# DLRM tower: first MLP layer spread over two steps, scale and offset at the turned copy, dense part of two blocks computed ahead

## The chip, the cores and the metric

The kernel runs on one core of a Trainium2 chip. Time is device time of one execution in microseconds (us), smaller is better. The core has TensorE (PE, with its weight loads as PEld), VectorE (DVE), ScalarE (ACT), GpSimd (POOL) and SyncE (SP), which only issues transfers here. Each engine works through its own instructions in the order in which they are written and waits on semaphores.

## The reference

A recommendation model on 512 samples, all in fp32. Cut to what matters (`ln` is layer norm over the last axis):

```
e = 26 table lookups per sample                              # [512, 26, 64]
x = ln(dense @ Wd.T) * gd + bd                               # [512, 128]
y = ln(e @ Ws.T) * gs + bs ; y = ln(y mixed by Wsi) * gsi + bsi   # 32 features of 128
T = [x, y]            ; Z = T @ T.T  (33 x 33 per sample), lower triangle
z = ln(Z_flat @ Wl.T) * gl + bl, the first 384 of 512 columns kept
h = relu([z, dense] @ W_top1 + b_top1)                       # 384 + 256 -> 512
h = relu(h @ W_top2 + b_top2)                                # 512 -> 256
out = h @ W_top3                                             # 256 -> 1
```

gl, bl and the biases are drawn, not ones and zeros.

## The kernel before

The 512 samples are 4 blocks of 128 (numbered k = 0 to 3, LAST = 3), and a block is 4 units of 16 pairs of samples, so there are 16 units, n = 0 to 15. GpSimd gathers the table rows of all units by 104 indirect transfers, six for a unit, eight for units 0, 4, 8 and 12. It waits for nothing but the indices.

All other engines run a software pipeline of steps n = 0 to 16, written out by hand. In step n TensorE does `transposes(n)` (L318) and `gram(n)` (L325), which give the row variances of unit n, `mix(n-1)` (L341) and `embed(n-1)` (L351) of the unit before, and `interact(n-2)` (L364, 32 small matmuls a unit). VectorE answers with L755 to L761 and L766 to L770 (`srow`, which `mix` waits for) and with L779 to L794 for the normalised T. ScalarE copies and squares between them; `interactions` (L595, L597) copies Z to `zs`. Z leaves through DRAM (L275 to L277) and comes back transposed (L241 to L250) before the block's `upper` layer, six matmuls of 512 columns called j = 0 to 5 (L381 to L386), can run. In fp32 every matmul is issued as two passes, which the profile counts one by one.

After `upper(k)`: `upper_norm` and `upper_scaled` (L614 to L622, the reciprocal L799 on VectorE) give `un`; `turn` (L392) transposes it on TensorE; `upper_turned` (L628) copies it as `znT`; `hidden1_dense` (L408, 8 matmuls) and `hidden1` (L422, in the last block L416, 12 matmuls) add up the first MLP layer in PSUM; `relu1` (L636), `hidden2` (L434), `relu2` (L642), `answer` (L444) follow. The scale gl is multiplied into W_top1 beforehand (`w1g`, L836), and the offset bl goes into the bias (`b1p`, L480 and L841), in step 6.

Where these stand is given by lags: `block_at(n, lag)` is block k when n = 4 k + lag, for blocks 0 and 1 alone. Their `upper` is in steps 4 k + 7 and 8, turn and first layer in 4 k + 9 (step 13 for block 1), second layer in 4 k + 10, answer in 4 k + 11. Blocks 2 and 3 are written out. `upper(2)` is cut over steps 15 and 16; what follows `interact(15)` is the tail:

```python
hidden1_dense(LAST - 1)
turn(LAST - 1)
hidden1_dense(LAST)
hidden1(LAST - 1)
upper(LAST, range(0, NL + 1))
hidden2(LAST - 1)
turn(LAST)
answer(LAST - 1)
hidden1(LAST)
```

`upper(3)` in it needs the last units' Z back from DRAM.

Of the kernel before, what the change touches and what calls it, by code (L numbers as in the profile page):

```python
# [11 lines left out]
P = 128  # L12
# [46 lines left out]
def build(nc, tables, index, consts, small, ws_t, gs_row, wsi_rows, dense_t, wd_t, wl, wlx, w1, w2, out):  # L59
# [3 lines left out]
    with ExitStack() as ctx:  # L63
# [55 lines left out]
        w1g = sb("w1g", [P, USED // P, H1])  # L119
        b1p = sb("b1p", [P, H1 // P])  # L120
# [75 lines left out]
        w1_ready, b1_done, b1_ready = map(sem, ["w1_ready", "b1_done", "b1_ready"])  # L196
# [111 lines left out]
        def _(pe):  # L308
# [59 lines left out]
            def upper(k, part):  # L368

                if part[0] == 0:  # L370
                    if k and k != LAST:
                        pe.wait_ge(h2_sb, H2 // P * k)
                    pe.wait_ge(zr_sb[k % 2], 16 * READS * (k // 2 + 1))
                    pe.wait_ge(xrow_sb, k + 1)
                    if k == 0:
                        pe.wait_ge(b1_ready, 1)
# [17 lines left out]

            def hidden1_dense(k):

                if k < LAST - 1:
                    pe.wait_ge(zT_sb, k + 1)
                else:
                    pe.wait_ge(t1_sb, 2 * NU)  # L400
                if k == LAST:
                    pe.wait_ge(zs_sb, NU)
                    pe.wait_ge(u_sb, LAST)
                if k == 0:
                    pe.wait_ge(w1_ready, 1)
                for c in range(USED // P, NK):
                    for m in range(H1 // P):
                        mm(hidden_part(k, m), w1_sb[:, c, P * m:P * (m + 1)], dense_sb[:, c - USED // P, P * k:P * (k + 1)],  # L408
                           start=c == USED // P and (m == 0 or k == LAST), stop=False, skip_group_check=True)

            def hidden1(k):
                pe.wait_ge(zT_sb, k + 1)
                if k == LAST:
                    for m in range(H1 // P):
                        for c in range(USED // P):
                            got = mm(hidden_part(k, m), w1g[:, c, P * m:P * (m + 1)], znT[:, c, :],  # L416
                                     start=False, stop=c == USED // P - 1, skip_group_check=True)
                        got.then_inc(h1_done, 1)
                else:
                    for c in range(USED // P):  # L420
                        for m in range(H1 // P):
                            got = mm(hidden_part(k, m), w1g[:, c, P * m:P * (m + 1)], znT[:, c, :],  # L422
                                     start=False, stop=c == USED // P - 1, skip_group_check=True)
                            if c == USED // P - 1:
                                got.then_inc(h1_done, 1)
# [48 lines left out]
            def hidden_bias():  # L474

                pe.wait_ge(ld_w1, 16 * NK)
                pe.wait_ge(w9_ready, 1)
                for m in range(H1 // P):
                    for c in range(USED // P):
                        got = mm(pU[:, m:m + 1], w1_sb[:, c, P * m:P * (m + 1)], col["bl"][:, c:c + 1],  # L480
                                 start=c == 0, stop=c == USED // P - 1)
                got.then_inc(b1_done, 1)

# [16 lines left out]
            for n in range(NU + 1):  # L500
# [16 lines left out]
                if (k := block_at(n, MLP)) is not None:  # L517
                    turn(k)
# [10 lines left out]
                if n == 6:  # L529
                    hidden_bias()  # L530
# [18 lines left out]
            upper(LAST, range(0, NL + 1))  # L549
            hidden2(LAST - 1)  # L550
# [7 lines left out]
        def _(act):  # L558
# [65 lines left out]
            def upper_turned(k):  # L624
# [3 lines left out]
                a.copy(znT[:], turn_bank(k)[:, 0:USED].rearrange("p (c n) -> p c n", n=P)).then_inc(zT_sb, 1)  # L628

            def relu1(k):  # L630
                if k == 0:
                    act.wait_ge(b1_ready, 1)
                for m in range(H1 // P):
                    if m == 0 or k == LAST:
                        act.wait_ge(h1_done, H1 // P * k + (m + 1 if k == LAST else H1 // P))
                    a.activation(h1[:, m, :], hidden_part(k, m), ACT.Relu, bias=b1p[:, m:m + 1]).then_inc(h1_sb, 1)  # L636
# [40 lines left out]
            for n in range(NU + 1):  # L677
# [12 lines left out]
                if (k := block_at(n, TOP)) is not None:  # L690
                    relu1(k)
# [6 lines left out]
                if n < NU:  # L698
                    row_deviation(n)
                if n == 0:  # L700
# [5 lines left out]
                if (k := block_at(n, MLP)) is not None:  # L706
                    upper_turned(k)
# [3 lines left out]
                if n >= 2:  # L711
                    interactions(n - 2)
                if (k := block_at(n, U0 - 1)) is not None:
# [17 lines left out]
            relu1(LAST - 1)  # L731
            upper_norm(LAST)
            upper_scaled(LAST)
            relu2(LAST - 1)
            upper_turned(LAST)
# [6 lines left out]
        def _(dve):  # L742
# [90 lines left out]
            def hidden_weights():  # L833
                dve.wait_ge(ld_w1, 16 * ((USED + DENSE) // P))
                for c in range(USED // P):
                    got = v.tensor_scalar(w1g[:, c, :], w1_sb[:, c, :], col["gl"][:, c:c + 1], None, ALU.mult)  # L836
                got.then_inc(w1_ready, 1)

            def hidden_bias():
                dve.wait_ge(b1_done, 1)  # L840
                v.tensor_tensor(b1p[:], pU[:, 0:H1 // P], col["b1"], ALU.add).then_inc(b1_ready, 1)  # L841
# [48 lines left out]
            for n in range(NU + 1):  # L890
                if n < NU:
                    row_variance(n)
                if (k := block_at(n, MLP)) is not None:
# [13 lines left out]
                if n == 6:  # L907
                    hidden_weights()
                    hidden_bias()
            upper_inverse(LAST - 1)  # L910
            upper_inverse(LAST)

# [66 lines left out]
```

## Time and profile before

| what | value |
|---|---|
| median of 3 runs | 182.81 us (182.76 to 183.86) |
| the profiled execution's own time | 184.26 us |
| its span | 182.5 us |
| mean granted TensorE clock | 0.972 |
| busy: PE / DVE / ACT / POOL | 146.5 / 117.0 / 86.0 / 106.0 us |
| last gather issued (L302) | ends 140.5 us from the start |

The span is what the trace covers, the profiled execution's own time lies 1.76 us above it, and the median of the runs without a profile is 1.45 us below that own time. Positions such as "at 166.29" are us from the start of the span. A timeline row gives start, duration, engine, line, operation, output and inputs, how many were merged in the row, and in brackets how long the engine had been idle before it and what ended that. A row of the page's groups gives line, engine, operation and count, then busy us and mean ns of one, then the idle time in front of them and what ended it.

### The profile page before, as it was taken

Reading aid. Unit: us, or ns where it says so; the run is one execution under the profiler, and the core shown is the slowest. Engines: PE = TensorE matmul, PEld = TensorE weight load, DVE = VectorE, ACT = ScalarE, POOL = GpSimd, SP = SyncE. Lnnn points to the kernel's source line nnn. Section 1 sums busy time; section 2 is a strip of 40 time slices with the busy share of each in tenths; the row PEclk is TensorE's granted clock in tenths of the full one; section 3 lists DMA queues with packets and bytes.
Section 4 is the critical chain, followed back from the end, with each engine's and each line's share of the span. In section 5 each row is a group of like instructions: output and inputs, shape, how many; then the busy total and the mean of one; then the engine's idle time right before and its main releaser. Section 6 shows DMA issues by size and latency. Waiting matters only on the chain.

```text
span 182.5 us, 4658 instructions
## 1 busy us (share of the span) xinstructions
PE 146.5 (80%) x1865; PEld 103.4 (57%) x1865; DVE 117.0 (64%) x279; ACT 86.0 (47%) x229; POOL 106.0 (58%) x108
## 2 busy tenths in 40 slices
PE   0475585648496989896996999699799999799995
PEld 0364263334162657764555977465497955497674
DVE  3798508797629899994869279939772996700000
ACT  3001333575425675773466176527634863712262
POOL 2778777787777777777777777777776000000000
PEclk9999969999969999799999999999999999999999
DMA  5613241325166653312136322212543103322000
GB/s 146 202 25 81 84 135 31 83 29 197 24 194 157 100 67 50 54 32 53 34 68 72 71 30 59 56 29 57 75 71 47 36 0 62 44 46 28 0 4 0
DMA packets 38520, 12.01 MB, mean 66 GB/s; under 512 B 34113, under 2 KB 35265, under 8 KB 38498
## 3 DMA queue, kind: packets, MB, share of 16 engines
q1 hardware_dynamic: 33586, 8.24, 20.6%
q0 software_dynamic: 3328, 3.41, 10.4%
q8 instruction: 15, 0.25, 0.5%
q10 hardware_dynamic: 1584, 0.05, 0.5%
q14 instruction: 7, 0.06, 0.1%
HBM read 9.46 MB, written 2.23 MB: 64 GB/s over the span
## 4 chain that ended last, share of the span: by engine, by line
POOL 51%; PE 20%; issue 16%; DMA 5%; DVE 3%; ACT 3%; SPq 1%; ACTq 0%; DVEq 0%
POOL rows L302 51%; PE pV L341 3%; PE pA L381 2%; PE pT L351 2%; PE pU L381 2%; DMA zr<-zscr 2%; DMA rows<-in_tables,idx 2%; PE pA L325 1%; PE pU L422 1%; PE pZ L364 1%; PE pU L408 1%; DMA idx_in<-in_index 1%; PE pU L434 1%; DMA zscr<-zs 1%; DVE T L794 1%
## 5 line engine op out<-in xcount | busy, mean ns | idle before, releaser
L302 POOL DMA_INDIRECT rows<-in_tables,idx x104 | 105.8, 1017 | 34.3 <-issue 31.4
L755 DVE TENSOR_TENSOR prod<-pA,rows 128x384 f32<-128x384 f32 (+1 forms) x16 | 9.4, 590 | 32.1 <-PE pA L325 32.1
L318 PE MATMUL pA<-const,rows 128*128 128x128 f32 x52 | 9.2, 294 | 18.3 <-DMA rows<-in_tables,idx 18.3
L794 DVE TENSOR_TENSOR T<-t,trs 128x512 f32<-128x512 f32 x32 | 22.2, 695 | 1.1
L583 ACT ACTIVATE t<-t 128x512 f32<-128x512 f32 x32 | 19.5, 629 | 6.2 <-DVE t L779 5.8
L341 PE MATMUL pV<-wexp,srow 128*64 128x192 f32 (+4 forms) x256 | 21.9, 317 | 0.0
L779 DVE TENSOR_TENSOR t<-pT,bias 128x512 f32<-128x512 f32 x32 | 20.5, 683 | 1.5 <-PE pT L351 1.4
L325 PE MATMUL pA<-gbd,rowsT 128*128 128x128 f32 x104 | 18.6, 326 | 3.5 <-ACT rowsT L566 3.4
L318 PEld LDWEIGHTS pA<-const,rows 128*128 128x128 f32 x52 | 5.9, 147 | 26.1 <-issue 23.2
L785 DVE TENSOR_REDUCE tss<-t 128x16 f32<-128x512 f32 x32 | 20.4, 677 | 0.1
L341 PEld LDWEIGHTS pV<-wexp,srow 128*64 128x64 f32 x256 | 16.5, 146 | 4.9 <-issue 3.3
L351 PE MATMUL pT<-vsb,wscg 64*128 64x512 f32 x64 | 19.0, 673 | 0.0
L325 PEld LDWEIGHTS pA<-gbd,rowsT 128*128 128x128 f32 x104 | 15.2, 222 | 6.6 <-ACT rowsT L566 4.3
L364 PEld LDWEIGHTS pZ<-T 128*32 128x32 f32 x1024 | 11.6, 109 | 11.5 <-issue 9.2
L566 ACT COPY rowsT<-pA 128x384 f32<-128x384 f32 (+1 forms) x16 | 7.9, 495 | 18.9 <-PE pA L318 18.9
L364 PE MATMUL pZ<-T 128*32 128x34 f32 x1024 | 13.7, 199 | 1.0 <-DVE T L794 1.0
L572 ACT ACTIVATE esd<-evar,eps 128x6 f32<-128x6 f32 (+1 forms) x16 | 4.8, 299 | 19.0 <-DVE evar L761 18.9
L588 ACT ACTIVATE tsd<-tss,eps 128x16 f32<-128x16 f32 x32 | 9.9, 308 | 6.9 <-DVE tss L785 6.6
L381 PE MATMUL pU<-wg,zr 128*128 128x512 f32 x24 | 13.0, 657 | 0.0
L578 ACT COPY vsb<-pV 128x512 f32<-128x512 f32 x16 | 9.4, 586 | 7.5 <-PE pV L341 7.1
L799 DVE RECIPROCAL urs<-usd 128x1 f32<-128x1 f32 x4 | 0.6, 160 | 14.4 <-ACT usd L616 14.3
L770 DVE TENSOR_TENSOR srow<-rows,ers 128x384 f32<-128x384 f32 (+1 forms) x16 | 9.5, 592 | 0.6
(153 smaller groups left out, 204.9 us busy)
## 6 DMA issues: line engine op xcount, KB each, us to landing
zscr<-zs SPq DMA_DIRECT2D x16, 128.0 KB
rows<-in_tables,idx POOLq DMA_INDIRECT x104, 2.6
wl_sb<-in_wl SPq DMA_DIRECT2D x5, 256.0 KB, 2.8
w_sb<-in_w SPq DMA_DIRECT2D x5, 256.0 KB, 3.4
dense_sb<-in_dense_t SPq DMA_DIRECT2D x1, 512.0 KB, 4.5
w_sb<-in_w SPq DMA_DIRECT2D x1, 512.0 KB
zr<-zscr SPq DMA_DIRECT2D x3, 96.0 KB
const<-in_consts SPq DMA_DIRECT2D x1, 263.0 KB, 2.9
```

The costliest lines, as they stand in the source:

```text
L302: pool.indirect_dma_start(out=rows[:, j, h * D:(h + 1) * D], out_offset=None, in_=tables, in_offset=bass.IndirectOffsetOnAxis(ap=idx[:, 2 ...
L318: got = nc.tensor.transpose(pA[n % 2][:, P * j:P * (j + 1)], rows[:, first + j, :], ident)
L325: got = mm(pA[n % 2][:, P * j:P * (j + 1)], rowsT[:, n % 2, j, :], gbd[:], start=True, stop=True)
L341: got = mm(pV[(n - m + u) % 2][D * h:D * (h + 1), PJ * (a - US * u):PJ * (z + 1 - US * u)], srow[:, n % 2, i, D * h:D * (h + 1)], wexp[:, ...
L351: mm(pT[h][:], wscg[D * h:D * (h + 1), :], vsb[D * h:D * (h + 1), n % 2, :], start=True, stop=True).then_inc(y_done, 1)
L364: got = mm(pZ[PJ * s:PJ * (s + 1), NCOL * g:NCOL * (g + 1)], t[:, h, i, 0:PJ], t[:, h, i, :], start=True, stop=True)
L381: mm(upper_bank(k)[:], zr[:, k % 2].rearrange("p a (g j) -> p (a g) j", j=4)[:, :, j], wg[:, j, :], start=j == 0, stop=False)
L583: a.activation(t2[:, h], t1[:, n % 2, h], ACT.Square).then_inc(t_sq, 1)
L588: a.activation(tsd[:, h], tss[:, h], ACT.Sqrt, bias=eps[:], scale=1.0 / PJ).then_inc(t_std, 1)
L779: v.tensor_tensor(t1[:, n % 2, h], pT[h][:].rearrange("p (a b) -> p a b", b=PJ), bias[:].unsqueeze(1).to_broadcast([P, US, PJ]), ALU.add). ...
L785: v.tensor_reduce(out=tss[:, h], in_=t2[:, h], op=ALU.add, axis=AX.X).then_inc(t_var, 1)
L794: v.tensor_tensor(tile_T(n)[:, h, :, 0:PJ], t1[:, n % 2, h], trs[:, h].unsqueeze(2).to_broadcast([P, US, PJ]), ALU.mult).then_inc(t_sb, 1)
```

## The change

1. **First layer, blocks 0 and 1.** `hidden1(k)` is cut: of the three 128-row chunks c of znT the first stays in step 4 k + 9 behind the dense part, the other two (8 matmuls) move to step 4 k + 10, between `gram` and `embed`. `turn(k)` goes behind `interact`. On ScalarE `upper_turned` goes behind `interactions`, and `relu1` behind `row_deviation`.
2. **Scale and offset.** `w1g` and `b1p` go, with the 12 small matmuls and the 4 VectorE instructions that made them. The copy to znT becomes three ScalarE activations of 128x128 with scale gl and offset bl (blocks 0 to 2), or three VectorE tensor_scalar (`last_turned`, block 3).
3. **Dense part of blocks 2 and 3.** It is computed in step 6 (`dense_ahead(0)` ahead of `embed(5)`, `dense_ahead(1)` behind `interact(4)`, 8 matmuls each) and stored in `hd`. VectorE adds it in four instructions a block (`hidden_sum`, to `hs`) between `hidden1` and `relu1`, which now reads `hs`.
4. **Order.** `hidden2(2)` goes ahead of `upper(3)`. Of `upper(2)`, step 15 has j = 0 in place of 0 and 1, step 16 has j = 1 ahead of `embed(15)` and 2 to 5 behind `interact(14)` in place of 2 ahead and 3 to 5 behind.

```diff
+            def dense_ahead(i):
+                k = LAST - 1 + i
+                if i == 0:
+                    pe.wait_ge(ld_w1, 16 * NK)
+                    pe.wait_ge(w9_ready, 1)
+                else:
+                    pe.wait_ge(hd_sb, 1)
+                for m in range(H1 // P):
+                    for c in range(USED // P, NK):
+                        got = mm(pU[:, P * m:P * (m + 1)], w1_sb[:, c, P * m:P * (m + 1)],
+                                 dense_sb[:, c - USED // P, P * k:P * (k + 1)], start=c == USED // P, stop=c == NK - 1)
+                got.then_inc(hd_done, 1)
...
+            def hidden1(k, part=range(USED // P)):
+                pe.wait_ge(zT_sb, k + 1)
+                if k == LAST - 1:
                     pe.wait_ge(t1_sb, 2 * NU)
...
+                if (k := block_at(n, TOP)) is not None:
+                    hidden1(k, [1, 2])
+                if n == 6:
+                    dense_ahead(0)
                 if n == NU:
-                    upper(LAST - 1, [2])
+                    upper(LAST - 1, [1])
...
-                if (k := block_at(n, MLP)) is not None:
-                    turn(k)
...
                 if n == 6:
-                    hidden_bias()
+                    dense_ahead(1)
...
                 if (k := block_at(n, MLP)) is not None:
+                    turn(k)
                     hidden1_dense(k)
-                    hidden1(k)
+                    hidden1(k, [0])
                 if n == NU - 1:
-                    upper(LAST - 1, [0, 1])
+                    upper(LAST - 1, [0])
                 if n == NU:
-                    upper(LAST - 1, [3, 4, 5])
+                    upper(LAST - 1, [2, 3, 4, 5])
             interact(NU - 1)
-            hidden1_dense(LAST - 1)
             turn(LAST - 1)
-            hidden1_dense(LAST)
             hidden1(LAST - 1)
+            hidden2(LAST - 1)
             upper(LAST, range(0, NL + 1))
-            hidden2(LAST - 1)
             turn(LAST)
...
-                a.copy(znT[:], turn_bank(k)[:, 0:USED].rearrange("p (c n) -> p c n", n=P)).then_inc(zT_sb, 1)
+                for c in range(USED // P):
+                    got = a.activation(znT[:, c, :], turn_bank(k)[:, P * c:P * (c + 1)], ACT.Identity,
+                                       bias=col["bl"][:, c:c + 1], scale=col["gl"][:, c:c + 1])
+                got.then_inc(zT_sb, 1)
...
+                if n == 6:
+                    act.wait_ge(hd_done, 1)
+                    a.copy(hd[:, 0, :], pU[:]).then_inc(hd_sb, 1)
...
+            def hidden_sum(k):
+                for m in range(H1 // P):
+                    dve.wait_ge(h1_done, H1 // P * k + (m + 1 if k == LAST else H1 // P))
+                    if k == LAST:
+                        dve.wait_ge(h1_sb, H1 // P * (k - 1) + m + 1)
+                    v.tensor_tensor(hs[:, P * m:P * (m + 1)], hidden_part(k, m),
+                                    hd[:, k - LAST + 1, P * m:P * (m + 1)], ALU.add).then_inc(hs_sb, 1)
+
+            def last_turned():
+                dve.wait_ge(zT_done, NBLK)
+                dve.wait_ge(h1_done, H1 // P * LAST)
                 for c in range(USED // P):
-                    got = v.tensor_scalar(w1g[:, c, :], w1_sb[:, c, :], col["gl"][:, c:c + 1], None, ALU.mult)
+                    got = v.tensor_scalar(znT[:, c, :], turn_bank(LAST)[:, P * c:P * (c + 1)], col["gl"][:, c:c + 1],
+                                          col["bl"][:, c:c + 1], ALU.mult, ALU.add)
+                got.then_inc(zT_sb, 1)
...
             upper_inverse(LAST - 1)
+            hidden_sum(LAST - 1)
             upper_inverse(LAST)
+            last_turned()
+            hidden_sum(LAST)
```

TensorE from `embed(12)` in step 13 to `hidden2(1)` in step 14, before (each row is a run of matmuls, output, inputs and shape, with their count):

```order
L351 MATMUL pT<-vsb,wscg 128x512 x2
L392 MATMUL pU<-const,un 128x128 x3
L364 MATMUL pZ<-T 32x34 x32
L408 MATMUL pU<-dense_sb,w_sb 128x128 x8
L422 MATMUL pU<-znT,w1g 128x128 x12
L318 MATMUL pA<-const,rows 128x128 x3
L341 MATMUL pV<-wexp,srow 64x192 x4
L341 MATMUL pV<-wexp,srow 64x96 x4
L325 MATMUL pA<-gbd,rowsT 128x128 x3
```

and changed (line numbers are those of the changed kernel, mostly higher by one):

```order
L352 MATMUL pT<-vsb,wscg 128x512 x2
L365 MATMUL pZ<-T 32x34 x32
L393 MATMUL pU<-const,un 128x128 x3
L415 MATMUL pU<-dense_sb,w_sb 128x128 x8
L432 MATMUL pU<-znT,w_sb 128x128 x4
L319 MATMUL pA<-const,rows 128x128 x3
L342 MATMUL pV<-wexp,srow 64x192 x4
L342 MATMUL pV<-wexp,srow 64x96 x4
L326 MATMUL pA<-gbd,rowsT 128x128 x3
L432 MATMUL pU<-znT,w_sb 128x128 x8
L352 MATMUL pT<-vsb,wscg 128x512 x2
```

Eight of the twelve first-layer matmuls now stand behind the step's gram and ahead of `embed(13)`; the turn stands behind the interactions.

TensorE in the tail, from `turn(2)` (into pV) to `turn(3)` (into pA), before:

```order
L392 MATMUL pV<-const,un 128x128 x3
L408 MATMUL pT<-dense_sb,w_sb 128x128
L408 MATMUL pV<-dense_sb,w_sb 128x128
L408 MATMUL pU<-dense_sb,w_sb 128x128
L408 MATMUL pZ<-dense_sb,w_sb 128x128
...
L422 MATMUL pT<-znT,w1g 128x128 x12
L381 MATMUL pA<-wg,zr 128x512 x4
L384 MATMUL pA<-wg,zr 128x512
L386 MATMUL pA<-w9c,z 128x512
L434 MATMUL pV<-h,w_sb 128x128 x8
L392 MATMUL pA<-const,un 128x128 x3
```

and changed:

```order
L393 MATMUL pV<-const,un 128x128 x3
L432 MATMUL pT<-znT,w_sb 128x128 x12
L445 MATMUL pV<-h,w_sb 128x128 x8
L382 MATMUL pA<-wg,zr 128x512 x4
L385 MATMUL pA<-wg,zr 128x512
L387 MATMUL pA<-w9c,z 128x512
L393 MATMUL pA<-const,un 128x128 x3
```

The dense matmuls are gone from it and the second layer of block 2 (L445) stands ahead of the upper layer of block 3.

VectorE at the end, changed, with what each row waits for (before, only the two reciprocals stood here):

```order
L808 RECIPROCAL urs<-usd 128x1 [waits u_std]
L848 TENSOR_TENSOR hs<-pT,hd 128x128 [waits h1_done] x4
L808 RECIPROCAL urs<-usd 128x1 [waits u_std]
L855 TENSOR_SCALAR znT<-pA,cols 128x128 [waits h1_done,zT_done]
L855 TENSOR_SCALAR znT<-pA,cols 128x128 x2
L848 TENSOR_TENSOR hs<-pT,hd 128x128 [waits h1_sb,h1_done]
```

The sum and the last turned copy are steps of VectorE between TensorE and what came next before.

## Rows read from the trace of the kernel before

**Rows 1.** The page: shares of the chain of waits, then the group of the transposes.

```profile
POOL 51%; PE 20%; issue 16%; DMA 5%; DVE 3%; ACT 3%; SPq 1%; ACTq 0%; DVEq 0%
...
L318 PE MATMUL pA<-const,rows 128*128 128x128 f32 x52 | 9.2, 294 | 18.3 <-DMA rows<-in_tables,idx 18.3
```

**Rows 2.** Timeline, TensorE, steps 13 to 15 (columns as told above).

```profile
126.53 0.52 PE L318 MATMUL pA<-const,rows 128*128 128x128 f32 x3 [0.31 <-DMA rows<-in_tables,idx]
...
133.05 2.05 PE L408 MATMUL pU<-dense_sb,w_sb 128*128 128x128 f32 x16 [0.20 <-ACT znT L628]
...
134.93 2.84 PE L422 MATMUL pU<-znT,w1g 128*128 128x128 f32 x24
...
137.61 0.49 PE L318 MATMUL pA<-const,rows 128*128 128x128 f32 x3
...
140.03 1.13 PE L351 MATMUL pT<-vsb,wscg 64*128 64x512 f32 x4
...
143.67 0.49 PE L318 MATMUL pA<-const,rows 128*128 128x128 f32 x3
```

**Rows 3.** Timeline, ScalarE in step 13 and VectorE in step 14.

```profile
132.53 0.46 ACT L628 COPY znT<-pU 128x384 f32<-128x384 f32 x1
...
141.40 1.29 DVE L779 TENSOR_TENSOR t<-pT,bias 128x512 f32<-128x512 f32 x2
```

**Rows 4.** Timeline, steps 15 and 16 up to `embed(15)`.

```profile
145.33 0.94 PE L325 MATMUL pA<-gbd,rowsT 128*128 128x128 f32 x6
...
146.31 0.56 DVE L755 TENSOR_TENSOR prod<-pA,rows 128x384 f32<-128x384 f32 x1
...
148.98 0.56 DVE L770 TENSOR_TENSOR srow<-rows,ers 128x384 f32<-128x384 f32 x1
...
150.40 1.14 PE L341 MATMUL pV<-wexp,srow 128*64 128x192 f32 x12
...
152.65 1.13 PE L351 MATMUL pT<-vsb,wscg 64*128 64x512 f32 x4
```

**Rows 5.** Timeline, step 16, end of `upper(2)` and ScalarE behind it.

```profile
155.49 1.02 PE L384 MATMUL pU<-wg,zr 128*128 128x512 f32 x2
...
156.34 1.02 PE L386 MATMUL pU<-w9c,z 128*128 128x512 f32 x2
...
159.20 0.32 ACT L595 COPY zs<-pZ 128x192 f32<-128x192 f32 x1
...
159.75 0.29 ACT L610 COPY z<-xsum 1x128 f32<-1x128 f32 x1
```

**Rows 6.** Timeline, the tail.

```profile
163.09 2.84 PE L422 MATMUL pT<-znT,w1g 128*128 128x128 f32 x24
...
165.97 1.14 ACT L636 ACTIVATE h<-pT,b1p 128x128 f32<-128x128 f32 x4 [3.99 <-PE pT L422]
...
166.29 3.82 PE L381 MATMUL pA<-wg,zr 128*128 128x512 f32 x8 [0.36 <-DMA zr<-zscr]
...
174.33 0.48 ACT L628 COPY znT<-pA 128x384 f32<-128x384 f32 x1
...
177.94 0.37 ACT L636 ACTIVATE h<-pZ,b1p 128x128 f32<-128x128 f32 x1 [0.30 <-PE pZ L416]
```

**Rows 7.** Timeline of the start: operations like the added ones, all from PSUM.

```profile
14.58 0.88 DVE L877 BATCH_NORM_STATS2 xstat<-pU 128x6 f32<-128x128 f32 x4
...
16.45 1.37 DVE L887 TENSOR_SCALAR xn<-pU,xmv,xrs 128x128 f32<-128x128 f32 x4
...
19.70 0.78 ACT L682 ACTIVATE xT<-pZ,cols 128x512 f32<-128x512 f32 x1 [3.02 <-PE pZ L451]
```

**Rows 8.** Busy time by window; columns PE, PEld, DVE, ACT, POOL, granted clock, DMA share, GB/s.

```profile
72.00:74.00 2.00, 1.34 (x12) 1.28 (x13) 1.97 (x6) 1.77 (x5) 1.39 (x3) 1.00 0.35 29
...
76.00:78.00 2.00, 2.00 (x8) 1.75 (x10) 2.00 (x6) 1.92 (x5) 1.57 (x2) 0.50 0.12 26
...
130.00:134.00 4.00, 2.74 (x77) 2.05 (x76) 3.93 (x10) 2.90 (x9) 3.08 (x4) 1.00 0.77 93
```

More of the change, by code:

```diff
@@ L118, in build @@
         wbraw = sb("wbraw", [P, UO])
-        w1g = sb("w1g", [P, USED // P, H1])
-        b1p = sb("b1p", [P, H1 // P])
+        hd = sb("hd", [P, 2, H1])
+        hs = sb("hs", [P, H1])
         xstat = sb("xstat", [P, NBLK, 6])
@@ L393, in turn @@
                 got.then_inc(zT_done, 1)
-            def hidden1_dense(k):
-                if k < LAST - 1:
-                    pe.wait_ge(zT_sb, k + 1)
-                else:
+            def dense_ahead(i):
[10 more added lines that the diff above has]
+                got.then_inc(hd_done, 1)
+            def hidden1_dense(k):
+                pe.wait_ge(zT_sb, k + 1)
+                for c in range(USED // P, NK):
+                    for m in range(H1 // P):
+                        mm(hidden_part(k, m), w1_sb[:, c, P * m:P * (m + 1)], dense_sb[:, c - USED // P, P * k:P * (k + 1)],
+                           start=c == USED // P and m == 0, stop=False, skip_group_check=True)
+            def hidden1(k, part=range(USED // P)):
+                pe.wait_ge(zT_sb, k + 1)
+                if k == LAST - 1:
                     pe.wait_ge(t1_sb, 2 * NU)
@@ L402, in hidden1_dense @@
                     pe.wait_ge(zs_sb, NU)
[L403 to L413, printed above, removed]
                     for m in range(H1 // P):
                         for c in range(USED // P):
-                            got = mm(hidden_part(k, m), w1g[:, c, P * m:P * (m + 1)], znT[:, c, :],
-                                     start=False, stop=c == USED // P - 1, skip_group_check=True)
+                            got = mm(hidden_part(k, m), w1_sb[:, c, P * m:P * (m + 1)], znT[:, c, :],
+                                     start=c == 0, stop=c == USED // P - 1)
                         got.then_inc(h1_done, 1)
                 else:
-                    for c in range(USED // P):
+                    for c in part:
                         for m in range(H1 // P):
-                            got = mm(hidden_part(k, m), w1g[:, c, P * m:P * (m + 1)], znT[:, c, :],
-                                     start=False, stop=c == USED // P - 1, skip_group_check=True)
+                            got = mm(hidden_part(k, m), w1_sb[:, c, P * m:P * (m + 1)], znT[:, c, :],
+                                     start=k == LAST - 1 and c == 0 and m == 0, stop=c == USED // P - 1,
+                                     skip_group_check=True)
                             if c == USED // P - 1:
@@ L472, in single_rows @@
                 mm(pU[96:97, :], bp64[32:64, :], wbraw[32:64, :], start=True, stop=True).then_inc(wrow_done, 1)
[L474 to L482, printed above, removed]
             pe.wait_ge(ld_const, 16)
@@ L689, in _ @@
                     upper_scaled(k)
-                if (k := block_at(n, TOP)) is not None:
-                    relu1(k)
                 if (k := block_at(n, ANS)) is not None:
                     relu2(k)
+                if n == 6:
+                    act.wait_ge(hd_done, 1)
+                    a.copy(hd[:, 0, :], pU[:]).then_inc(hd_sb, 1)
                 if n in (5, 6, 7):
@@ L699, in _ @@
                     row_deviation(n)
+                if (k := block_at(n, TOP)) is not None:
+                    relu1(k)
                 if n == 0:
@@ L705, in _ @@
                     squares(n - 1)
-                if (k := block_at(n, MLP)) is not None:
-                    upper_turned(k)
                 if (k := block_at(n, ANS)) is not None:
@@ L712, in _ @@
                     interactions(n - 2)
+                if (k := block_at(n, MLP)) is not None:
+                    upper_turned(k)
                 if (k := block_at(n, U0 - 1)) is not None:
@@ L831, in single_rows @@
                 v.tensor_copy(w9[96:97, :], pU[96:97, :]).then_inc(w9_ready, 1)
-            def hidden_weights():
-                dve.wait_ge(ld_w1, 16 * ((USED + DENSE) // P))
-                for c in range(USED // P):
-                    got = v.tensor_scalar(w1g[:, c, :], w1_sb[:, c, :], col["gl"][:, c:c + 1], None, ALU.mult)
[L837 to L841, printed above, removed]
+            def hidden_sum(k):
+                for m in range(H1 // P):
+                    dve.wait_ge(h1_done, H1 // P * k + (m + 1 if k == LAST else H1 // P))
[6 more added lines that the diff above has]
+                dve.wait_ge(h1_done, H1 // P * LAST)
+                for c in range(USED // P):
+                    got = v.tensor_scalar(znT[:, c, :], turn_bank(LAST)[:, P * c:P * (c + 1)], col["gl"][:, c:c + 1],
+                                          col["bl"][:, c:c + 1], ALU.mult, ALU.add)
+                got.then_inc(zT_sb, 1)
             v.memset(eps[:], EPS)
@@ L892, in _ @@
                     row_variance(n)
+                if n == 7:
+                    dve.wait_ge(hd_done, 2)
+                    v.tensor_copy(hd[:, 1, :], pU[:]).then_inc(hd_sb, 1)
                 if (k := block_at(n, MLP)) is not None:
```

22 lines of the change are left out of this document (10 added, 12 removed).

## The prediction

> **What bounds the kernel now.** I read the chain of waits first. It is GpSimd for half of the span, with TensorE second [rows 1]: up to step 13 the gathers set the pace. The group of the transposes shows the same from TensorE's side, since its steps waited 18.3 us in all for gathered rows [rows 1]. The last such wait is the 0.31 us ahead of step 13, at 126.53 [rows 2]. What comes later in step 13 or after is no longer hidden behind a gather, what comes earlier mostly is.
>
> Then the timeline from there. Step 13 carries the whole first MLP layer of block 1, 40 passes from 133.05 to 137.61, so that step 14 starts at 137.61 and step 15 at 143.67 with no wait in front of them [rows 2]: here TensorE's own list is the bound. In step 15 VectorE's `srow` is ready at 148.98 + 0.56 = 149.54, but `mix(15)` starts at 150.40, behind two matmuls of `upper(2)` [rows 4]. In step 16 TensorE finishes `upper(2)`, ScalarE norms and scales it, and only then, at 159.20, copies the last unit's Z to `zs` [rows 5], though Z has been there for a little while. That copy starts the round trip through DRAM, whose end releases `upper(3)` at 166.29, after 0.36 us of idle TensorE [rows 6]. So `un` of block 2 is in front of the round trip on ScalarE, and what TensorE does during the trip (turn, both dense parts, first layer of block 2) is hidden. `hidden2(2)` stands behind `upper(3)` and runs while ScalarE norms block 3, so that it is hidden as well. From 173.8 on the last block's MLP is one chain.
>
> **The change, part by part.** All times below are shifts against the profiled execution.
>
> *Early steps.* Step 6 gets 32 passes of dense work and two copies of 128x512, and a wait of TensorE for `w9_ready` and of ScalarE for the first eight matmuls; 24 passes and four VectorE instructions go. At 0.11 us a pass (2.68 us for 24, from 134.93 to 137.61 [rows 2]) that is 3.6 us at most for step 6, against 18.3 us of waits for gathers [rows 1], of which several lie between steps 6 and 13. Block 0's layer is spread over steps 9 and 10, again ahead of step 13. I cost both at nothing; if the cover failed, the 0.31 us at 126.53 would be the first to go, and each later 0.1 us would count in full.
>
> *Step 13, znT.* The copy to znT started at 132.53 [rows 3]. It now stands behind the two `zs` copies; such a pair takes 0.55 us (159.20 to 159.75 [rows 5]), starting where znT did. Then come three activations with scale and offset as operands in place of one plain copy of 0.46 us. Lower bound: `relu1`, four of 128 columns with one such operand, 1.14 us, one of them 0.37 [rows 6], so 0.26 for each further one and 0.37 + 2 x 0.26 = 0.89 for three. Upper: the same operation on 512 columns took 0.78 us [rows 7], three times that 2.3. I take 1.16: the nearer row is `relu1`, and a second operand makes each a little longer, 0.09 by my estimate, since 0.78 is 0.2 above what 512 columns with none would take by the slope of the copies. So znT is ready at 132.53 + 0.55 + 1.16 - 0.07 (overlap) = 134.17, not 132.99: **+1.17**.
>
> *Steps 13 and 14, TensorE.* 16 passes leave step 13: 16 x 0.11 = 1.79. Step 14 starts at 137.61 + 1.17 - 1.79 = 137.0. The gather for it was there, and the turn, moved behind `interact`, fills idle time and gains nothing, because ScalarE's znT sets what follows. The same 1.79 come back between `gram(14)` and `embed(13)`, so `embed(13)` starts at 140.03 + 1.17 = 141.2 and step 15 at 143.67 + 1.17 = 144.84. Queued behind the moved matmuls are `embed(13)` and with it VectorE's L779 at 141.40 [rows 3], which moves by about 1.0: it was 0.15 us later than TensorE asked. From there VectorE is back to back to the product of step 15, 146.31 [rows 4], which moves by 1.0 too.
>
> *Step 15.* `srow` ends at 149.54 + 1.03 = 150.57. TensorE comes with `upper(2)` cut to one matmul, two passes of 0.43 (0.85 for two, 155.49 to 156.34 [rows 5]): 150.40 + 1.17 - 0.86 = 150.7. So `mix(15)` starts at 150.7, **+0.3**; the shorter `upper` pays for most of the delay. Between it and `embed(15)` there is one matmul of `upper` as before, so `embed(15)` is at 152.95.
>
> *Step 16.* Behind `interact(14)` stand four matmuls in place of three: +0.86 for the end of `upper(2)`, and as ScalarE is in order, +0.3 + 0.86 = **+1.16** for `zs` (159.20 to 160.36 [rows 5]) and for the return of Z, 166.29 to 167.45.
>
> *TensorE during the round trip.* From `zs` on: 0.55 and 0.29 us for its two copies and the copy of L610 [rows 5], 161.2; three activations, 162.3; `hidden1(2)`, 2.88 us from its start to the first relu (163.09 to 165.97 [rows 6]), 165.2; the first sum of VectorE, then `relu1`, 1.14 [rows 6]; then `hidden2(2)`, 16 passes, 1.88 (133.05 to 134.93 [rows 2]). The price of one sum is between 0.22 (a quarter of the 0.88 for four reads of 128 columns from PSUM [rows 7], were they all overlapped) and 0.56 (the product of 384 columns [rows 4]); I take 0.28 and 0.04 to be released, by the first. That gives 165.2 + 0.32 + 1.14 + 1.88 = 168.6 for the start of `upper(3)`. Z is back at 167.45, so the MLP of block 2 and not the transfer is late: **+2.3** against 166.29. The dense matmuls that left were hidden and give nothing.
>
> *Last block.* `upper(3)`, norm and turn are unchanged. The turned copy was 0.48 us of ScalarE [rows 6]; three tensor_scalar of 128 columns from PSUM with two operands are by [rows 7] (four in 1.37) about 0.4 + 2 x 0.32 = 1.05: **+0.57** (with the faster reads of the same rows, 0.66 and +0.2). The Trainium skill has a rule here (VectorE: DVE Perf Modes, The TRN2 errata): each VectorE instruction from PSUM pays a fixed part besides its elements, so that small tiles pay it each time. By its table one such instruction is an estimated 0.26 us, three +0.3 and the sum 0.27 smaller; the row, 0.34 each, is dearer, and I go by the row. Of the four sums only the last is on the chain (the others hide under 0.67 us of matmuls each): **+0.32**, ahead of the relu at 177.94 [rows 6].
>
> *Sum.* 2.3 + 0.57 + 0.32 = **+3.2 us**. That is 184.26 + 3.2 = 187.5 for the profiled execution, which stood 1.45 above the median; against the median 182.81 it is **186.0 us**. Since my takes lean to the dear side at the two activations, I name 185.9.
>
> **The forecast's own bounds.** Cheap activations (0.27 less, twice) and cheap instructions on VectorE (0.4 and 0.1 less) leave +2.2, 185.0. Activations at 0.5 apiece (0.34 more for three, twice) and sums at 0.5 (0.2 more, twice) make it +4.3, 187.1.
>
> **The rivals.**
>
> *The transfer hides `hidden2(2)`.* If ScalarE gets to znT sooner than I think, or the way of Z back is slower by 1 us because its stores leave at another moment, `upper(3)` starts with its data at about 167.4: +1.1 + 0.9 = +2.0, 184.8 us. For it: Z's return waits for a transfer with no fixed time. Against: the gap to close is 1.15 us.
>
> *The early steps give time, and there is no loss.* The change takes two matmuls' time from in front of `mix(15)`, and a wait in front of the turn (TensorE idle between `embed(12)` and the turn). If step 15 could start when its rows have landed, some 1.1 us sooner than 143.67, and `mix(15)` took the 0.86 too, `embed(15)` would be 1.9 earlier: `zs` -1.9 + 0.86 = -1.0, the return of Z at 165.3, the MLP of block 2 done 7.7 later than `zs`, 165.9; with the cheap VectorE prices, 0.2 + 0.2 on the last block, the sum is 0.0: 182.8 us. It decides from the point where `embed(13)` starts no later than 140.0; the 16 passes placed ahead of it speak against that, and it holds only if ScalarE's znT is at 132.9 or sooner. A part of this gives 183.5.
>
> *TensorE's clock falls in the tail.* In the window 76 to 78 it was granted 0.50, its lower level of 1.2 GHz, after a stretch where it was busy for 1.34 of 2.0 us [rows 8]. In the changed tail it is idle for about 1.2, 1.2 and 1.5 us between 159 and 167 (waiting for `un`, for znT, and for sums and relu), where before it was busy nearly throughout. If `upper(3)` ran at the lower level, its 5.4 us would double: 191.4 us. Against: from 130 to 134 it was busy for 2.74 of 4.0 us and granted 1.00 [rows 8], its upper level of 2.4 GHz, and the waits of the changed tail are no larger in share than that until 166. The Trainium skill states the same mechanism (TensorE: Matmul & The Clock Gate, The HAM clock gate): too little activity halves the clock until matmuls have run again. By that rule the case is open, not excluded.
>
> **Chances.** Forecast 0.58, transfer hides it 0.16, no loss 0.18, clock 0.08. A measurement tells 1%, here 1.8 us, from no change: above 184.64 is slower. The forecast lies above it but for a small tail, the transfer case for about half, the no-loss case is within 1% for 0.13 and faster for 0.05, clock is slower. Together: slower 0.71, within 1% 0.24, faster 0.05. The range from 183.6 to 187.3 leaves out the clock case, the far end of the forecast and the better part of the no-loss case.
>
> **What would show it.** Step 14's transposes near 137.0 and step 15's near 144.8 (the first layer's split costs 1.2 us); `mix(15)` near 150.7; `zs` near 160.4; `upper(3)` released not by the transfer but by TensorE's own `hidden2(2)`, near 168.6; from there to the end 0.9 us more than before; and 1.00 granted in all windows from 126 on. The prediction is wrong if step 13 no longer waits for its gather, if `upper(3)` still waits for Z, or if the three small activations take much less than 0.9 us.

## The result and the profile after

| kernel | median | runs | ratio to before |
|---|---|---|---|
| before | 182.78 us | 181.73 to 183.86 | |
| changed | 190.4 us | 187.86 to 191.01 | 1.0326 [1.0260, 1.0393] |

The change costs 6.0 us by the ratio (4.8 to 7.2); 3.1 were forecast, with 187.3 as the top of the range. Some runs of a kernel are slower as a whole than its others (of the changed kernel 190.79, the profiled one, and 191.01), and every ratio here leaves them out, while a median has all runs. Where two kernels are compared below, "by the ratios" means the difference of their ratios times the 182.8 us of before. The profiles are compared over stretches that begin with step 13, so that the time ahead of it does not enter.

The page of the changed kernel, in the form of [rows 1]:

```profile
PE 49%; POOL 20%; issue 10%; ACT 9%; DVE 8%; DMA 4%; ACTq 0%
...
L319 PE MATMUL pA<-const,rows 128*128 128x128 f32 x52 | 9.5, 301 | 8.2 <-DMA rows<-in_tables,idx 8.2
```

TensorE has taken GpSimd's place on the chain, and its steps wait 8.2 instead of 18.3 us for gathers, all of it ahead of step 6. TensorE's timeline, steps 13 to 16, against [rows 2, 4]:

```profile
125.74 0.49 PE L319 MATMUL pA<-const,rows 128*128 128x128 f32 x3
...
130.62 0.55 PE L393 MATMUL pU<-const,un 128*128 128x128 f32 x3
133.25 3.62 PE L415 MATMUL pU<-dense_sb,w_sb 128*128 128x128 f32 x16 [2.08 <-ACT znT L631]
136.66 1.16 PE L432 MATMUL pU<-znT,w_sb 128*128 128x128 f32 x8
137.66 0.49 PE L319 MATMUL pA<-const,rows 128*128 128x128 f32 x3
...
141.86 1.13 PE L352 MATMUL pT<-vsb,wscg 64*128 64x512 f32 x4
...
145.51 0.49 PE L319 MATMUL pA<-const,rows 128*128 128x128 f32 x3
...
151.33 1.14 PE L342 MATMUL pV<-wexp,srow 128*64 128x192 f32 x12
```

Step 13 has no wait for its gather any more, one of the signs that the prediction had named for being wrong. TensorE then stands idle for 2.08 us for znT, and the 16 dense passes behind that take 3.41 us to the next row instead of 1.88. Its tail, against [rows 6]:

```profile
162.99 2.94 PE L432 MATMUL pT<-znT,w_sb 128*128 128x128 f32 x24 [1.37 <-ACT znT L631]
167.63 2.05 PE L445 MATMUL pV<-h,w_sb 128*128 128x128 f32 x16 [1.69 <-ACT h L643]
169.52 3.72 PE L382 MATMUL pA<-wg,zr 128*128 128x512 f32 x8
...
176.87 0.55 PE L393 MATMUL pA<-const,un 128*128 128x128 f32 x3 [1.92 <-ACT un L624]
...
178.56 1.65 PE L426 MATMUL pT<-znT,w_sb 128*128 128x128 f32 x6 [0.62 <-DVE znT L855]
180.00 1.49 PE L426 MATMUL pV<-znT,w_sb 128*128 128x128 f32 x6
```

`upper(3)` is no longer released by the transfer: it follows `hidden2(2)`. Behind the norm of block 3 TensorE is idle for 1.92 us, and then each matmul group of block 3's first layer takes 1.28 to 1.44 us to the start of the next instead of 0.67 to 0.78. Windows of the changed kernel, with the columns of [rows 8]:

```profile
130.00:134.00 4.00, 1.80 (x36) 1.35 (x24) 3.49 (x8) 3.59 (x11) 3.05 (x4) 0.93 0.76 104
134.00:138.00 4.00, 4.00 (x25) 3.91 (x24) 1.35 (x3) 0.00 (x0) 1.90 (x2) 0.64 0.29 45
...
174.00:178.00 4.00, 2.03 (x10) 0.69 (x8) 0.70 (x3) 1.58 (x5) 0.00 (x0) 0.98 0.00 0
178.00:182.00 4.00, 3.44 (x16) 3.44 (x17) 1.09 (x4) 0.79 (x3) 0.00 (x0) 0.50 0.00 0
```

The granted clock falls to its lower level (1.2 GHz) in both places, each time after a stretch in which TensorE is busy for half the time, 1.80 and 2.03 of 4.0 us. The added operations, on ScalarE and VectorE:

```profile
132.03 1.17 ACT L631 ACTIVATE znT<-pU,cols 128x128 f32<-128x128 f32 x3
...
160.92 0.31 ACT L597 COPY zs<-pZ 128x192 f32<-128x192 f32 x1
...
165.97 0.89 DVE L848 TENSOR_TENSOR hs<-pT,hd 128x128 f32<-128x128 f32 x4 [5.57 <-PE pT L432]
...
177.46 1.05 DVE L855 TENSOR_SCALAR znT<-pA,cols 128x128 f32<-128x128 f32 x3 [1.26 <-PE pA L393]
```

They cost what the sum said: 1.17 us for three activations (1.16 taken), 1.05 for three tensor_scalar (1.05), and the relu starts 0.33 after the first sum (0.32).

### The profile page after: what moved, and what is told of

It is laid out like the page before. It is cut to its first block, busy times and chain, and to the rows that moved or that the text cites. A ratio compares the mean times of both kernels' runs of the same rounds, so it can differ in the third digit from the quotient of the medians.

```text
span 189.0 us, 4627 instructions
## 1 busy us (share of the span) xinstructions
PE 152.8 (81%) x1841; PEld 108.0 (57%) x1841; DVE 120.5 (64%) x287; ACT 87.2 (46%) x235; POOL 101.7 (54%) x108
## 3 DMA queue, kind: packets, MB, share of 16 engines
q0 software_dynamic: 3328, 3.41, 9.9%
## 4 chain that ended last, share of the span: by engine, by line
PE 49%; POOL 20%; issue 10%; ACT 9%; DVE 8%; DMA 4%; ACTq 0%
POOL rows L303 20%; PE pV L342 7%; PE pU L382 6%; PE pA L326 4%; PE pT L352 4%; PE pU L415 3%; PE pU L432 3%; PE pZ L365 3%; DMA rows<-in_tables,idx 3%; PE pU L445 2%; PE pU L406 2%; PE pA L382 2%; PE pA L319 2%; ACT znT L631 2%; PE pT L432 2%
## 5 line engine op out<-in xcount | busy, mean ns | idle before, releaser
L303 POOL DMA_INDIRECT rows<-in_tables,idx x104 | 101.5, 976 | 34.2 <-issue 31.4
L352 PE MATMUL pT<-vsb,wscg 64*128 64x512 f32 x64 | 19.9, 701 | 0.0
L365 PEld LDWEIGHTS pZ<-T 128*32 128x32 f32 x1024 | 12.2, 112 | 13.0 <-issue 10.5
L319 PE MATMUL pA<-const,rows 128*128 128x128 f32 x52 | 9.5, 301 | 8.2 <-DMA rows<-in_tables,idx 8.2
L319 PEld LDWEIGHTS pA<-const,rows 128*128 128x128 f32 x52 | 6.8, 156 | 15.6 <-issue 13.7
L365 PE MATMUL pZ<-T 128*32 128x34 f32 x1024 | 14.7, 203 | 0.2 <-DVE T L803 0.2
L415 PE MATMUL pU<-dense_sb,w_sb 128*128 128x128 f32 x32 | 6.5, 386 | 4.2 <-ACT znT L631 4.2
```

The lines of the kernel that those rows point to most:

```text
L303: pool.indirect_dma_start(out=rows[:, j, h * D:(h + 1) * D], out_offset=None, in_=tables, in_offset=bass.IndirectOffsetOnAxis(ap=idx[:, 2 ...
L319: got = nc.tensor.transpose(pA[n % 2][:, P * j:P * (j + 1)], rows[:, first + j, :], ident)
L352: mm(pT[h][:], wscg[D * h:D * (h + 1), :], vsb[D * h:D * (h + 1), n % 2, :], start=True, stop=True).then_inc(y_done, 1)
L365: got = mm(pZ[PJ * s:PJ * (s + 1), NCOL * g:NCOL * (g + 1)], t[:, h, i, 0:PJ], t[:, h, i, :], start=True, stop=True)
```

## The experiments

Theory: the added instructions and waits cost the 3.2 us of the sum, and the rest is TensorE's clock, which falls because the new order leaves TensorE idle. Rival: the rest, too, lies in the added instructions and waits themselves, and the clock only accompanies it.

The first table holds the measured ratios to the kernel before. The second has, for each kernel's profiled execution, starts counted from the start of step 13 (its L318 or L319 row; 126.53 before, 125.74 changed), then the time from turn(3) to the end of the span, and from step 13 to that end.

| kernel | median us | ratio [95%] |
|---|---|---|
| E1 fillers everywhere | 186.06 | 1.0188 [1.0127, 1.0249] |
| E2 fillers in steps 9, 13 | 188.01 | 1.0243 [1.0163, 1.0323] |
| E3 fillers in the tail | 189.99 | 1.0237 [1.0146, 1.0328] |
| E4 order of steps 9, 13 undone | 189.23 | 1.0313 [1.0234, 1.0392] |
| E5 E1, hidden2(2) late | 183.58 | 1.0039 [1.0004, 1.0073] |
| E6 dense back in the tail | 189.18 | 1.0274 [1.0200, 1.0348] |
| E7 before, upper(2) cut anew | 182.31 | 0.9970 [0.9939, 1.0000] |
| E8 E7, zs ahead of un | 182.07 | 0.9958 [0.9928, 0.9988] |
| E9 changed, hidden2(2) late | 187.22 | 1.0207 [1.0136, 1.0277] |
| E10 E4 and E9 | 185.31 | 1.0134 [1.0063, 1.0204] |
| E11 before, hidden2(2) early | 186.72 | 1.0194 [1.0132, 1.0257] |
| E12 E11 with fillers | 185.17 | 1.0138 [1.0064, 1.0212] |

| kernel | step 15 | zs | upper(3) | turn(3) to end | step 13 to end |
|---|---|---|---|---|---|
| before | 17.14 | 32.67 | 39.76 | 8.75 | 55.97 |
| sum of the prediction | 18.31 | 33.83 | 42.1 | 9.6 | 59.2 |
| changed | 19.77 | 35.18 | 43.78 | 12.13 | 63.26 |
| E1 | 18.17 | 33.58 | 42.18 | 9.52 | 59.05 |
| E2 | 18.17 | 33.59 | 43.81 | 11.13 | 62.29 |
| E3 | 19.78 | 35.19 | 43.80 | 9.55 | 60.70 |
| E4 | 17.82 | 33.24 | 43.46 | 11.20 | 62.01 |
| E5 | 18.26 | 33.67 | 40.08 | 9.51 | 57.02 |
| E6 | 19.77 | 35.18 | 44.33 | 11.94 | 63.62 |
| E7 | 17.24 | 32.75 | 39.50 | 8.71 | 55.66 |
| E8 | 17.14 | 31.87 | 39.29 | 8.69 | 55.44 |
| E9 | 19.70 | 35.11 | 41.59 | 9.60 | 58.59 |
| E10 | 17.83 | 33.24 | 39.72 | 9.58 | 56.71 |
| E11 | 17.30 | 32.84 | 42.69 | 10.03 | 60.08 |
| E12 | 17.14 | 32.67 | 42.53 | 8.64 | 58.52 |

**E1 to E3, TensorE kept busy.** A filler is a matmul of the identity with itself into a bank that nobody reads at that time. The first edit (E1, E2) is for steps 9 and 13, the second (E1, E3) stands in the tail, and likewise with 6, 7, 8 and 2 in its other four waits.

```diff
                     turn(k)
+                    pe.wait_ge(e_mul, n)
+                    keep_busy(pA[(n + 1) % 2], 8)
                     hidden1_dense(k)
...
+            keep_busy(pV[1], 4)
             turn(LAST - 1)
```

> The changed kernel with idle TensorE filled: matmuls of 128x128 that nobody reads, 8 between the turn and the dense part in steps 9 and 13, and 4, 6, 7, 8 and 2 in the five waits of the tail (before turn(2), hidden1(2), hidden2(2), turn(3), hidden1(3)). Clock theory: the loss beyond my 3.2 us is TensorE at its lower level after idle stretches (133 to 136.6 and 178 to 185 in the changed kernel's trace). With 1.00 granted from 96 on, it comes to 185.0 to 186.5 us, near my forecast, and 4.3 to 5.5 us below the changed kernel. Rival, the added instructions between the engines are the loss: the clock accompanies but costs nothing, and it stays at 189 to 192 us.

> Only the 8 matmuls in steps 9 and 13. Clock theory: the 24 passes at 133.25 to 137.66 take 2.7 instead of 4.4 us, step 14 starts 1.6 us sooner, and the end moves by that, 1.3 to 2.5 us below the changed kernel (187.9 to 189.1); the tail still falls to the lower level. Rival: no change, 190 us or more.

> Only the fillers of the tail. Clock theory: hidden1(3) takes 2.7 instead of 5.3 us and hidden2(3) 0.4 less, so about 3.0 us below the changed kernel, 187 to 188; step 13 still falls. Rival: no change, 190 us or more.

E1 is the decisive one: with 43 matmuls added and nothing taken away it is faster than the changed kernel, by 2.5 us by the ratios (4.3 in the medians), and the intervals do not meet. In its profile the stretch from step 13 is 59.05 us, where the sum had 59.2 and the changed kernel has 63.26. Its windows over the two places:

```profile
134.00:138.00 4.00, 4.00 (x43) 3.64 (x42) 0.77 (x3) 1.06 (x2) 3.09 (x4) 1.00 0.34 47
...
178.00:182.00 4.00, 3.45 (x27) 2.56 (x25) 0.58 (x2) 1.89 (x6) 0.00 (x0) 1.00 0.00 0
```

The rival, which had 189 to 192 us and no gain, falls. E2 and E3 each restore their own place in the table (step 15 at 18.17; turn to end 9.55) and leave a fall in the other. E2 also shows that the falls move about. The wait for znT in its tail, 1.36 us, is as long as the changed kernel's 1.37, but here the clock falls behind it:

```profile
159.66 4.57 PE L437 MATMUL pT<-znT,w_sb 128*128 128x128 f32 x24 [1.36 <-ACT znT L638]
```

4.57 instead of 2.94 us, which delays `hidden2(2)` and `upper(3)` by 1.6. So the 1.6 us won in step 13 are lost again at `upper(3)` (43.81 against 43.78), and the 1.0 us that E2 gains from step 13 on comes from the last layer, where the lower level ended sooner (11.13 against 12.13). E3 gains 2.56 us from step 13 on, but 1.6 by the ratios, with intervals that meet, and its median missed my range by 2 us; its runs are spread over 6 us. Its profile (192.63) shows where time can go ahead of step 13: behind waits of 3.42 us in step 5 and 1.66 in step 6 TensorE was granted 0.50 (60 to 64 and 74 to 76), the first dense part took 3.38 instead of the changed kernel's 2.02, no later step waited for its gather, and step 13 started at 130.10. The profiles of E5 and E9, with step 13 at 128.38 and 129.51, have the same two falls.

**E4, order of steps 9 and 13.**

```diff
+                if (k := block_at(n, MLP)) is not None:
+                    turn(k)
                 if (k := block_at(n, ANS)) is not None:
                     answer(k)
...
                     squares(n - 1)
+                if (k := block_at(n, MLP)) is not None:
+                    upper_turned(k)
```

> The changed kernel with the order of steps 9 and 13 undone: turn ahead of answer and interact, the three activations to znT straight behind the squares; the first layer stays spread over two steps. TensorE then waits for znT for about 0.5 to 0.8 us instead of 2.1, since interact fills the rest. Clock theory: no fall of the clock at 133, and the wait itself is shorter by 0.5: 1.8 to 2.6 us below the changed kernel (187.8 to 188.6). Rival: the wait's 0.5 us alone, 189.9.

The place behaves as expected: two waits of 1.06 and 1.03 us with `interact` between them in place of one of 2.08, the dense passes at full speed, step 15 sooner by 1.95.

```profile
130.91 0.55 PE L393 MATMUL pU<-const,un 128*128 128x128 f32 x3 [1.06 <-ACT un L625]
...
133.19 2.05 PE L415 MATMUL pU<-dense_sb,w_sb 128*128 128x128 f32 x16 [1.03 <-ACT znT L632]
```

The time does not, 189.2 us, 0.6 above the range, since the tail's falls stay, one of them now on the path of `upper(3)` as in E2: 0.32 us are left there of the 1.95, and with a shorter fall over the last layer (11.20) the stretch from step 13 is 1.25 us shorter. By the ratios (1.0313 and 1.0326) E4 can't be told from the changed kernel.

**E5, E9, hidden2(2) behind upper(3) again,** in the filled and in the plain changed kernel. On ScalarE relu2(2) goes back with it, and in E5 the eight fillers ahead of turn(3) go.

```diff
-            hidden2(LAST - 1)
             upper(LAST, range(0, NL + 1))
+            hidden2(LAST - 1)
```

> The filled kernel (fillers in steps 9 and 13 and in the tail) with hidden2(2) and relu2(2) put back behind upper(3), where before had them; the eight fillers ahead of turn(3) go, since hidden2(2) takes their place. In the filled kernel Z is back at about 165.0 (issue at 160.84 plus the 4.1 us that it took before) and upper(3) starts at 166.73. If TensorE's hidden2(2) and not the transfer is what upper(3) waits for, it starts 1.0 to 1.8 us sooner and the time is 184.3 to 185.1 us. Rival (the transfer is late, hidden2(2) is hidden): 186 us, no change.

> The changed kernel with hidden2(2) and relu2(2) put back behind upper(3), no fillers. My theory now: the order of hidden2(2) costs twice, 2 us because Z waits for it, and up to 3 us because TensorE then idles 1.9 us ahead of turn(3) and runs the last layer at its lower level. With it undone, upper(3) starts some 2 us sooner, the last layer is granted 1.00, and the time is 184.5 to 187 us; step 13 still falls. Rival (the fall in the tail comes from the dense part being absent, or from the waits before hidden1(2)): 188 to 189.

E5 against E1: `upper(3)` 2.10 us sooner, the medians 2.5 apart, intervals apart. I had allowed for 1.0 to 1.8, and the median is 0.7 us below the range. E9 against the changed kernel: `upper(3)` 2.2 sooner, and the last layer at full speed without a filler, since `hidden2(2)` stands in the norm's wait:

```profile
176.42 1.95 PE L445 MATMUL pV<-h,w_sb 128*128 128x128 f32 x16
178.50 0.55 PE L393 MATMUL pA<-const,un 128*128 128x128 f32 x3
...
180.20 0.94 PE L426 MATMUL pT<-znT,w_sb 128*128 128x128 f32 x6 [0.42 <-DVE znT L855]
```

4.67 us less from step 13 on. By the ratios it is 2.2 us, with intervals that still meet, and the median of 187.22 is just above the range.

**E6, the dense part back in the tail.** Part 3 of the change is undone, everything else stays.

```diff
             interact(NU - 1)
+            hidden1_dense(LAST - 1)
             turn(LAST - 1)
+            hidden1_dense(LAST)
             hidden1(LAST - 1)
             hidden2(LAST - 1)
...
-            hidden_sum(LAST - 1)
```

> The changed kernel without its part 3 and without fillers: the dense parts of blocks 2 and 3 are computed in the tail again and added up in PSUM, no sum by VectorE; step 6 has nothing of them. If computing them ahead is what left TensorE idle in the tail, the tail is granted 1.00 throughout, each layer loses the 0.32 us of the sum, and the time is 187 to 188.5 us; step 13 still falls to the lower level. Rival (the dense work in the tail costs more than its absence): 190 us or more.

Wrong: the median is 0.7 us above the range, and by the ratios E6 can't be told from the changed kernel. The dense work fills the wait before `hidden1(2)`, but not the one that counts, ahead of `turn(3)`:

```profile
179.46 0.55 PE L394 MATMUL pA<-const,un 128*128 128x128 f32 x3 [1.92 <-ACT un L629]
...
181.15 1.65 PE L433 MATMUL pT<-znT,w_sb 128*128 128x128 f32 x6 [0.52 <-DVE znT L854]
```

So it is not the work computed ahead that brings the last fall. What is left is the order of `hidden2(2)`, which E9 to E12 try.

**E10, both orders undone.** The edits of E4 and E9 together.

> As the one before, and the order of steps 9 and 13 undone too (turn ahead of interact, znT behind the squares). Then neither place leaves TensorE idle for over 1.5 us; what is left is the late zs (+1), the sum and the copy of the last block (+0.7): 183.5 to 185 us. Rival: over 186, if other falls of the clock remain.

Step 13 to end is 56.71, 0.74 more than before, and the two expected terms are there: `zs` +0.57, turn to end +0.83. The late `zs` costs nothing, as `upper(3)` is at 39.72, 6.5 us behind `zs` instead of 7.1. The median is 0.3 us above the range, and its ratio is worth 2.5 us: the rest of it lies ahead of step 13 or in the profiled execution of before, which stood 1.45 above its median. That is not settled.

**E11, E12, the order of hidden2(2) alone, on the kernel before.** The diff of E9 in the other direction; E12 adds `keep_busy(pT[0], 8)` ahead of `turn(LAST)`.

> The kernel before with one part of the change: hidden2(2) and relu2(2) ahead of upper(3). The first layer of block 2 ends at 165.9, relu1 at 167.1, hidden2(2) at 169.0, so upper(3) starts 2.7 us later than 166.3 and the norm of block 3 has nothing beside it. My theory: +2.7 and a fall of the clock over the last layer, +1.5 to +3: 187 to 188.5 us. Rival (order alone): 185.5.

> As the one before, with 8 matmuls of 128x128 that nobody reads between upper(3) and turn(3). The clock holds, the delay of upper(3) stays: 185.2 to 186 us. If it equals the one without fillers, the clock in that place costs nothing.

`upper(3)` starts 2.9 and 2.8 us later than before (2.7 expected). Without and with fillers, turn(3) and the first group behind it:

```profile
175.37 0.59 PE L392 MATMUL pA<-const,un 128*128 128x128 f32 x3 [1.92 <-ACT un L622]
...
176.83 1.65 PE L416 MATMUL pT<-znT,w1g 128*128 128x128 f32 x6
```

```profile
173.96 0.55 PE L397 MATMUL pA<-const,un 128*128 128x128 f32 x3
...
175.07 0.94 PE L421 MATMUL pT<-znT,w1g 128*128 128x128 f32 x6
```

The same idle 1.92 us, the same fall, 1.39 us by the table, in a kernel that has nothing else of the change. The medians agree (1.5 us apart), though their intervals overlap, so for the size the rows stand. E11's median is just under its range. Its ratio is worth 3.6 us (2.4 to 4.7): this one order by itself costs the kernel before over half of what the whole change costs.

**E7, E8, what can be kept.** The kernel before with the new cut of `upper(2)`, and in E8 ScalarE's `interactions(15)` ahead of `upper_scaled(2)`.

```diff
-                    upper(LAST - 1, [0, 1])
+                    upper(LAST - 1, [0])
...
-            upper_scaled(LAST - 1)
             interactions(NU - 1)
+            upper_scaled(LAST - 1)
```

> The kernel before with one thing of the change: upper(2) has j = 0 in step 15, 1 ahead of embed(15), 2 to 5 behind interact(14). mix(15) starts 0.8 us sooner (srow is ready at 149.54, before it started at 150.40), but u_done comes at the same time and zs waits behind un on ScalarE: no measurable change, 182.5 to 183.1 us. If mix(15) were bound elsewhere: 183.5.

> As the one before, and ScalarE copies the last unit's Z to zs ahead of upper_scaled(2), so that the round trip no longer stands behind un. zs then follows interact(15) at once, 0.8 us sooner than in the kernel before: 181.8 to 182.2 us, faster by about 0.4 per cent. Rival (zs gains nothing, since T of unit 15 is not sooner): 182.8.

```profile
157.13 0.32 ACT L595 COPY zs<-pZ 128x192 f32<-128x192 f32 x1
...
157.46 0.60 ACT L622 ACTIVATE un<-pU,urs 128x384 f32<-128x384 f32 x1
...
164.55 3.82 PE L381 MATMUL pA<-wg,zr 128*128 128x512 f32 x8 [0.69 <-DMA zr<-zscr]
```

`zs` is 0.80 us sooner in E8 than before, `upper(3)` 0.47, and the kernel is faster than before by 0.4% (0.1 to 0.7). E7 alone lies at the edge of what can be told (0 to 0.6%), its median is 0.2 us under its range, and E7 and E8 can't be told apart.

## Why the prediction was wrong

**The sum was right for a TensorE at its upper level, the chance of the clock was not.** Step by step against E1, where the clock holds: step 15 at 18.31 forecast, 18.17 measured; `mix(15)` 24.17 and 23.99; `zs` 33.83 and 33.58; `upper(3)` 42.1 and 42.18; turn to end +0.89 forecast, +0.77 measured. E1's median of 186.06 stands at the 185.9 that I named for the changed kernel, and its ratio is worth 3.4 us against a sum of 3.2.

**Failed: the step "1.00 granted in all windows from 126 on".** The sum priced every matmul behind its new waits at the upper level; in the changed kernel the 16 dense passes of step 13 took 3.41 instead of 1.88 us, and the groups of block 3's first layer 1.28 to 1.44 instead of 0.67 to 0.78. The rival that had it, "TensorE's clock falls in the tail", was given 0.08. The reason it was put low, that the window 130 to 134 was granted 1.00 with 2.74 of 4.0 us busy [rows 8], was read from the wrong kernel. In that window the changed kernel is busy for 1.80. The sum itself contained the wait: znT 1.17 us later with the turn done sooner is an idle stretch of 2.1 us, which I named as "gains nothing" and did not carry to the clock. I also placed the fall on `upper(3)`, priced at 5.4. It came in two other places: 1.6 us in step 13 (E1 or E2 against the changed kernel, step 15 at 18.17 and 19.77) and 2.6 over the last layers (12.13 and 9.52), 4.2 together in these profiles. By the ratios the changed kernel is 2.5 us (not 4.2) above E1. The falls move about (E2), so a smaller share in the other runs would fit, but they have no traces, and that is not shown.

**Thinner than read: the cover of the early steps.** The sum put step 6 against 18.3 us of waits for gathers. Of these only 4.5 lie in steps 7 to 13 of the kernel before (0.66, 1.52, 0.42, 1.59 and 0.31 in steps 7, 8, 9, 12 and 13), and the changed kernel has none left from step 6 on. Its step 6:

```profile
64.82 0.55 PE L319 MATMUL pA<-const,rows 128*128 128x128 f32 x3
...
69.89 2.02 PE L406 MATMUL pU<-dense_sb,w_sb 128*128 128x128 f32 x16 [1.73 <-DVE w L840]
...
73.80 1.96 PE L406 MATMUL pU<-dense_sb,w_sb 128*128 128x128 f32 x16
75.59 0.49 PE L319 MATMUL pA<-const,rows 128*128 128x128 f32 x3
```

The step takes 10.8 us where it took 7.1 before (66.15 to 73.21, without its wait for the next gather), 1.73 of them for `w9_ready` (L840), the wait that the prediction names and puts at nothing. The clock fell in step 9 as well (0.66 from 100 to 104): steps 9 and 10 took 20.0 us, against 18.2 in E1 with its fillers.

What this costs at the end is not settled. Step 13 begins with a wait for its gather in three of the five profiles with the old steps 6 and 9 (before, E8, E12) and in one of the nine with the new ones or parts of them (E1). In before, E7, E8, E11 and E12 it starts at 124.1 to 126.5, in E1, E2, E4 and E10 at 124.0 to 126.5, with gathers of much the same speed, so there I can't show a cost. The changed kernel's profile had the quickest gathers (976 ns in the mean, 995 in E2) and still started step 13 at 125.74, 1.7 us behind E2, which fits a fall in step 9 that nothing covered. No kernel had the new step 6 alone.

**A small misreading.** Z of the last unit had not been there for a while at 159.20: `interact(15)` ran from 158.39 to 159.16. In the changed kernel it ends at 160.10 and `zs` starts at 160.92, so there ScalarE's `un` does hold `zs` back.

**Right: "the transfer hides hidden2(2)" does not hold.** It is worth 2.1 us (E5 against E1), and with the wait it leaves in front of turn(3) it is the dearest part of the change: 4.7 us from step 13 on in E9's profile, and 3.6 us by E11's ratio. **Right: the prices of the small operations.** The table of the Trainium skill (VectorE: DVE Perf Modes, The TRN2 errata) would have had an estimated 0.8 us for the three tensor_scalar; they took 1.05, so the row decides.

**Right: the loss is not undone by the shorter upper in step 15.** Alone it is worth some 0.3% (E7, 0 to 0.6%).

## What to carry to other kernels

Work that fills a wait of TensorE off the critical path still had a use here: it kept the clock up for what came next. Before moving such work, read from the order which waits it leaves uncovered, add up idle and busy time there in the changed order, and price every matmul behind a half-idle stretch at both clock levels. A work item that is ready early (here `hidden2(2)`) belongs in the longest wait of a later chain (here the norm), not ahead of the matmuls that a transfer releases.

## What the runs showed of the hardware

The same idle time does not always bring the fall: the wait of 1.4 us ahead of `hidden1(2)` left the clock at its upper level in the changed kernel and was followed by the lower one in E2, E4, E9 and E10, where the 24 passes took 4.57 instead of 2.9 us. In E9 and E10 that cost next to nothing, as `upper(3)` stands 6.48 us behind `zs` in both, against 6.41 in E5, where the clock held. The wait of 1.92 us ahead of `turn(3)` was followed by it in all five profiles that leave it unfilled (changed, E2, E4, E6, E11). The Trainium skill says that a long wait for a DMA between matmuls lets the clock drop (TensorE: Matmul & The Clock Gate, Loop structure matters more than you think). These traces agree that waits do it, and show it behind waits of 1.4 to 2.1 us for ScalarE, with short groups of matmuls between them.

GpSimd's gathers wait for nothing but the indices, yet their mean was 1017 ns before, 976 ns in the changed kernel and 993 to 1019 in E1 to E12, which is up to 4 us over 104 of them. It follows none of the edits: E4 and E10 (1014 and 1019 ns) have most of the change. Before, 21 gathers took more than 1.05 us, in the changed kernel 11; why was not tried.
